# Softmax attention on TensorE: full 128-row products against two 64-row halves in two PSUM banks, with transposes moved between them

## The chip, the cores and the metric

One core of a Trainium2 chip runs the whole kernel, which is one launch of a two-layer transformer. The metric is the device time in microseconds (us), lower is better. The kernel before took 1138.88 us as the median of three runs (1138.76 to 1141.35).

## What is computed

The reference is two layers on 1024 tokens of width 256: softmax attention with 16 heads (4 key/value heads), a squared-relu mixture of experts, linear attention, and a silu mixture of experts, each with a layer norm ahead and a residual sum behind. The change is in the first of the four:

```
xq = (x @ wq + bq).reshape(B, S, 16, 128)
xk = (x @ wk + bk).reshape(B, S, 4, 128);  xv = (x @ wv + bv).reshape(B, S, 4, 128)
attn = softmax(einsum('bqhgd,bkhd->bhgqk', (xq / sqrt(128)).reshape(B, S, 4, 4, 128), xk))
out = einsum('bhgqk,bkhd->bqhgd', attn, xv).reshape(B, S, 2048)
return out @ wo + bo
```

## The kernel before

`softmax_attention_phase` (L223) goes through the four key/value heads one after another, a lap each. Every product is made in float32 precision out of three float32r products of high and low parts: `product` (L37) issues high x high (L39), high x low (L40) and low x high (L41).

Inside a lap the work is written as a list of events, which every engine walks in the same order and takes its own part of:

- `("q", h)` is the projection of one query head, `("k",)` and `("v",)` those of keys and values, `("y", b)` the output projection of half of the tokens.
- `("s", n)` is half of a tile of scores: 128 queries by 512 keys (L521). Two of them fill a slot of two PSUM banks. VectorE then takes the maximum (L686), ScalarE the exponential into `prob` (L579), VectorE the reciprocal of the sum (L647), and GpSimd multiplies by it (L422).
- `("t", n)` is one step of transposing the probabilities: four transposes of 128x128 from four tiles into one PSUM bank (L531 to L539). ScalarE copies the bank to `pt_h` (L612), VectorE subtracts that from the bank and gets the low part `pt_l` (L697).
- `("p", n)` adds one block of 128 keys to the outputs of 512 queries (L540): three products with `v` as weights and `pt` streaming. After eight of them the output unit is copied to `o_h` (L622) and `o_l` (L703).

A lap has 64 steps of each of s, t and p. The scores run 12 steps ahead of the rest (`LEAD`). The steady part of the list (L252 to L259) is a period of s, s, p, p, t, t, repeated, with a `q` ahead of every eighth pair; in it t is 4 steps ahead of p. Behind it follows `change` (L261), the passage to the next head with its k, v and y, or `closing` (L266) in the last lap.

What holds the engines together are semaphores. `turned(j)` (L325) gives the transposes two banks, one for a step, so a step waits until the one before the last is split (L535). `pt_h` and `pt_l` are rings of four steps (`PT`), so ScalarE's copy of step n waits until `("p", n - 4)` is done (L611). The slots of scores are two in the laps; a slot is free for the next scores when its exponential is done. The wait counts on `pt_split` and `pv_done` have `LIFT` added, which is given to the semaphore at the start.

## Time and profile before

| | |
|---|---|
| median of three runs | 1138.88 us |
| the profiled execution, its own time | 1144.78 us |
| its span (first to last instruction) | 1142.9 us |
| mean granted TensorE clock | 0.973 |
| TensorE products busy (6276 instructions) | 1059.6 us, 93% |
| weight loads busy | 893.9 us, 78% |
| VectorE, ScalarE, GpSimd busy | 751.3, 599.2, 564.3 us |
| the attention's transposes, first and last start | 40.8 and 602.4 us |

The span is some 2 us shorter than the execution's own time, and that is 5.9 us above the median. The attention takes roughly the first 610 us of the span. Start times in the rows are us from the start of the span. A product's record is longer than the distance to the next one, since products are pipelined: what a product costs in a dense row of them is read from start to start.

### The profile page before, as it was taken

What the parts mean: (1) busy time and instruction counts of PE and PEld (TensorE: products, weight loads), DVE (VectorE), ACT (ScalarE), POOL (GpSimd) and SP (SyncE); (2) the same over time, 40 slices, a digit from 0 to 9 for tenths busy, and PEclk for the clock granted to TensorE, in tenths of its full rate; (3) what the DMA queues carried; (4) which work ended last, traced back from release to release, by engine and by line L of the source; (5) the groups of instructions that cost most, each with busy time, mean ns of one, the idle gap of its engine ahead of it and who ended that gap; (6) DMA issues with size and microseconds to landing.
All of it is one profiled execution on the core that took longest, in us unless ns stands there. A gap on an engine that the chain in (4) does not pass through costs nothing. (4 is left out here: it accounts for less than half of the span.)

```text
span 1142.9 us, 16866 instructions
## 1 busy us (share of the span) xinstructions
PE 1059.6 (93%) x6276; PEld 893.9 (78%) x6276; DVE 751.3 (66%) x1312; ACT 599.2 (52%) x1027; POOL 564.3 (49%) x408
## 2 busy tenths in 40 slices
PE   5899999999999999999998899997977978999992
PEld 4788888888888888888886776654755778999992
DVE  4877665777457775667775644446778765777777
ACT  3566654666446665456662424333422255777772
POOL 1664623756136563355540347772314776644453
PEclk9999999999999999999999899999988998999997
DMA  8400210002501672000001146631200457666665
GB/s 198 49 29 1 54 40 1 19 10 46 48 1 40 209 216 52 1 1 1 1 1 39 43 146 217 212 125 55 106 2 5 157 190 239 205 226 222 224 208 203
DMA packets 45634, 109.84 MB, mean 96 GB/s; under 512 B 8519, under 2 KB 26069, under 8 KB 43504
## 3 DMA queue, kind: packets, MB, share of 16 engines
q1 hardware_dynamic: 38640, 95.46, 29.1%
q0 software_dynamic: 6912, 13.30, 3.1%
q8 instruction: 50, 0.82, 0.3%
q14 instruction: 32, 0.26, 0.1%
HBM read 94.27 MB, written 41.29 MB: 119 GB/s over the span
## 5 line engine op out<-in xcount | busy, mean ns | idle before, releaser
L422 POOL TENSOR_TENSOR at_prob<-at_prob,at_inv_sum 128x1024 f32<-128x1024 f32 x128 | 243.6, 1905 | 286.4 <-DVE at_inv_sum L647 286.4
L612 ACT ACTIVATE at_pt_h<-ps 128x512 fp32r<-128x512 f32 x256 | 139.1, 596 | 152.4 <-PE ps L537 152.3
L697 DVE TENSOR_TENSOR at_pt_l<-ps,at_pt_h 128x512 fp32r<-128x512 f32 x256 | 164.6, 685 | 64.5 <-ACT at_pt_h L612 64.5
L686 DVE TENSOR_REDUCE at_neg_max<-ps 128x1 f32<-128x1024 f32 x128 | 154.7, 1209 | 36.3 <-PE ps L41 35.9
L579 ACT ACTIVATE at_prob<-ps,at_neg_max 128x1024 f32<-128x1024 f32 x128 | 143.6, 1122 | 17.9 <-DVE at_neg_max L686 17.9
L537 PE MATMUL ps<-ident,at_prob 128*128 128x128 f32 x1024 | 133.8, 274 | 3.8 <-POOL at_prob L422 3.8
L2072 POOL DMA_INDIRECT lines<-f_y,f_x_raw x96 | 97.1, 1011 | 81.0 <-ACT f_y L1990 51.9
L537 PEld LDWEIGHTS ps<-ident,at_prob 128*128 128x128 f32 x1024 | 120.1, 141 | 21.1 <-POOL at_prob L422 4.7
L39 PE MATMUL ps<-at_k_h,at_q_h 128*128 128x512 f32 x256 | 109.0, 426 | 0.0
L39 PE MATMUL ps<-at_pt_h,at_v_h 128*128 128x512 f32 x256 | 101.1, 395 | 0.0
L41 PE MATMUL ps<-at_pt_h,at_v_l 128*128 128x512 f32 x256 | 100.8, 394 | 0.0
L41 PE MATMUL ps<-at_k_h,at_q_l 128*128 128x512 f32 x256 | 100.8, 394 | 0.0
L40 PE MATMUL ps<-at_k_l,at_q_h 128*128 128x512 f32 x256 | 100.6, 393 | 0.0
L40 PE MATMUL ps<-at_pt_l,at_v_h 128*128 128x512 f32 x256 | 100.2, 392 | 0.0
L1023 POOL TENSOR_TENSOR f_act<-f_act,f_cw_row 128x1024 f32<-128x1024 f32 x32 | 77.5, 2424 | 35.8 <-DVE f_act L1058 29.2
L1058 DVE SCALAR_TENSOR_TENSOR f_act<-ps,f_relu 128x1024 f32<-128x1024 f32 x34 | 41.6, 1223 | 57.2 <-ACT f_relu L964 57.2
L964 ACT ACTIVATE f_relu<-ps 128x1024 f32<-128x1024 f32 x36 | 36.8, 1022 | 72.4 <-PE ps L41 72.4
L39 PE MATMUL ps<-f_x_h,f_e_h 128*128 128x384 f32 (+1 forms) x192 | 67.1, 349 | 3.9 <-DVE f_x_l L2188 2.0
L41 PE MATMUL ps<-f_x_h,f_e_l 128*128 128x384 f32 (+1 forms) x192 | 64.8, 338 | 0.0
L40 PE MATMUL ps<-f_x_l,f_e_h 128*128 128x384 f32 (+1 forms) x192 | 64.8, 337 | 0.0
L2059 POOL DMA_INDIRECT slots<-f_row,f_slot_of x48 | 51.1, 1065 | 20.1 <-issue 13.1
L926 PE MATMUL ps<-f_act,f_e_raw 128*128 128x512 f32 x128 | 59.7, 593 | 0.0
(308 smaller groups left out, 2546.7 us busy)
## 6 DMA issues: line engine op xcount, KB each, us to landing
e_raw<-in_we SPq DMA_DIRECT2D x32, 624.0 KB, 4.2
f_cw_row<-cw SPq DMA_DIRECT2D x32, 512.0 KB, 3.9
slots<-in_empty SPq DMA_DIRECT2D x4, 3456.0 KB, 43.9
f_x_raw<-slots SPq DMA_DIRECT2D x32, 432.0 KB, 4.8
lines<-in_empty SPq DMA_DIRECT2D x3, 2048.0 KB, 32.8
f_e_raw<-in_we SPq DMA_DIRECT2D x32, 128.0 KB, 2.2
at_wq_raw<-in_wq SPq DMA_DIRECT2D x4, 512.0 KB, 3.7
at_wo_raw<-in_wo SPq DMA_DIRECT2D x4, 512.0 KB, 3.5
```

Source lines behind the costliest of these rows:

```text
L39: nc.tensor.matmul(out, lhs_h, rhs_h, start=start, stop=False)
L40: nc.tensor.matmul(out, lhs_h, rhs_l, start=False, stop=False)
L41: return nc.tensor.matmul(out, lhs_l, rhs_h, start=False, stop=stop)
L422: nc.gpsimd.tensor_tensor(prob[:, t % RING, :], prob[:, t % RING, :], inv_sum[:, t:t + 1].broadcast_to([P, T]), ALU.mult).then_inc(normed, 1)
L537: last = nc.tensor.transpose(turned(e[1])[:, i * P:(i + 1) * P], prob[:, (4 * u + i) % RING, kt * P:(kt + 1) * P], net.ident[:, :])
L579: nc.scalar.activation(halves(prob[:, t % RING, :]), slot(k, start), ACT.Exp, bias=neg_max[:, t:t + 1], accum_out=row_sum[:, t:t + 1]).the ...
L612: nc.scalar.activation(pt_h[:, e[1] % PT, :], turned(e[1]), ACT.Copy).then_inc(pt_high, 1)
L686: nc.vector.tensor_reduce(neg_max[:, t:t + 1], slot(n, start), AX.XY, ALU.max, negate=True).then_inc(maxed, 1)
L697: nc.vector.tensor_tensor(pt_l[:, e[1] % PT, :], turned(e[1]), pt_h[:, e[1] % PT, :].bitcast(F32), ALU.subtract).then_inc(pt_split, 1)
L926: last = nc.tensor.matmul(ps[:, 4 + b, :], e_raw[:, m, 1, :], act_of(m)[:, cols], start=first, stop=final)
L1023: nc.gpsimd.tensor_tensor(act_of(r), act_of(r), cw_row[:, r % ROWS, :], ALU.mult).then_inc(weighed, 1)
L2072: nc.gpsimd.indirect_dma_start(out=net.lines, out_offset=bass.IndirectOffsetOnAxis(ap=line_of, axis=0), in_=y[:, n % YRING, b, :], in_offs ...
```

## The change

Every attention product in the laps is taken apart into two halves of its contraction: rows 0 to 63 and rows 64 to 127 of weights and of what streams. `half_products` issues the halves in pairs, one on each half of the rows, into two different PSUM banks; in the first turn half 0 goes to bank 0 and half 1 to bank 1, in the second turn crosswise. The second turn waits until the first one is done (`halved`). One `s` event is now one turn over a whole tile of 1024 keys, one `p` event one turn over two steps, each with 256 of the queries in a bank; q, k, v and y in the laps are split into a first turn and a rest `("r", ...)`. The transposes read 64 rows each: eight to a step, each with 64 columns of the identity streaming, and bank `h` gets the queries of half `h` for both steps of a pair. So a bank is whole only after the second step of a pair, and the first step waits until both banks of the pair before are split. The ring `pt` is still four steps, now as two pairs. The steady period becomes s, t, s, p, t, p. The finished outputs go through `o_full` in SBUF.

The core of the diff (bare ... lines mark what is left out):

```diff
+HROWS = P // 2
+def upper(r):
+    return slice(r * HROWS, (r + 1) * HROWS)
+def half_products(nc, turn, outs, lhs_h, lhs_l, rhs_h, rhs_l, start, stop):
+    passes = [(lhs_h, rhs_h), (lhs_h, rhs_l), (lhs_l, rhs_h)]
+    for n, (lhs, rhs) in enumerate(passes):
+        for r in range(2):
+            j = r ^ turn
+            last = nc.tensor.matmul(outs[j], lhs[j][upper(r)], rhs[j][upper(r)], start=start and turn == 0 and n == 0,
+                                    stop=stop and turn == 1 and n == len(passes) - 1)
+    return last
...
+    def woven(a, b):
+        return [a[0], b[0], a[1], b[1]]
+    def query(s):
+        return ("q", (s // 2 + 2) // TT) if (s // 2 + 2) % TT == 0 and s < STEPS else None
+    opening = [("k",), ("q", 0), ("v",), ("s", 0)]
+    for s in range(2, LEAD, 2):
+        opening += [("s", s), ("s", s - 1)]
+    opening += [("s", LEAD - 1), ("vs",)] + pair("t", 0)
+    steady = woven([query(LEAD), rest(*query(LEAD))], pair("s", LEAD))
     for s in range(LEAD, STEPS, 2):
-        if (s // 2 + 2) % TT == 0:
-            steady.append(("q", (s // 2 + 2) // TT))
-        steady += pair("s", s)
+        ahead = query(s + 2)
+        begun, ended = ([ahead], [rest(*ahead)]) if ahead else ([], [])
+        turn = pair("t", s - LEAD + 2)
         if s > LEAD:
-            steady += pair("p", s - LEAD - 2)
-        steady += pair("t", s - LEAD + 2)
+            (s0, s1), (p0, p1) = pair("s", s), pair("p", s - LEAD - 2)
+            steady += [s0, turn[0], s1, p0] + begun + [turn[1], p1] + ended
+        else:
+            steady += begun + turn + ended
...
-    change = [("k",)] + pair("p", at) + pair("t", at + 4) + [("v",)] + pair("p", at + 2) + pair("t", at + 6)
+    change = woven([("k",), rest("k")], pair("p", at)) + pair("t", at + 4)
+    change += woven([("v",), rest("v")], pair("p", at + 2)) + pair("t", at + 6)
     for n in range(3):
-        change += pair("s", 2 * n) + pair("p", at + 4 + 2 * n) + pair("t", at + 8 + 2 * n)
-    change += pair("s", 6) + pair("p", at + 10) + pair("s", 8) + pair("p", at + 12)
-    change += [("vs",)] + pair("s", 10) + [("y", 0)] + pair("t", 0) + [("y", 1)]
+        change += woven(pair("s", 2 * n), pair("p", at + 4 + 2 * n)) + pair("t", at + 8 + 2 * n)
+    change += woven(pair("s", 6), pair("p", at + 10)) + woven(pair("s", 8), pair("p", at + 12))
+    change += [("vs",)] + pair("s", 10) + [("y", 0)] + pair("t", 0) + [rest("y", 0), ("y", 1), rest("y", 1)]
     closing = []
     for n in range(at, STEPS, 2):
-        closing += pair("p", n) + (pair("t", n + 4) if n + 4 < STEPS else [])
+        closing += woven(pair("p", n), pair("t", n + 4)) if n + 4 < STEPS else pair("p", n)
...
-        pt_h, pt_l = sb("pt_h", [P, PT, BANK], F32R), sb("pt_l", [P, PT, BANK], F32R)
+        pt_h, pt_l = sb("pt_h", [P, PT // 2, 2, BANK], F32R), sb("pt_l", [P, PT // 2, 2, BANK], F32R)
         o_h, o_l = sb("o_h", [P, PER, T], F32R), sb("o_l", [P, PER, T], F32R)
+        o_full = sb("o_full", [P, BANK])
...
-        def turned(j):
-            return ps[:, 4 + j % 2, :]
-        def o_bank(u):
-            return ps[:, 6 + u % 2, :]
+        def turned(h):
+            return ps[:, 4 + h, :]
+        def stored(pt, step):
+            return pt[:, step // 2 % (PT // 2), step % 2, :]
+        def moving(pt, step):
+            return [pt[:, step // 2 % (PT // 2), h, step % 2 * D:(step % 2 + 1) * D] for h in range(2)]
+        def queries(ap):
+            return ap.rearrange("p (i h q) -> p h i q", i=4, h=2)
+        def outputs(h):
+            return ps[:, 6 + h, 0:D]
+        def all_outputs():
+            return ps[:, 6:8, 0:D].rearrange("p h (i q) -> p h i q", i=4)
...
+                        if turn:
+                            pe.wait_ge(halved, halves_of[g, job])
+                            place_ = slot(slot_of[job], start)
...
-                            keys = slice(b * BANK, (b + 1) * BANK)
-                            last = product(nc, slot(n, start)[:, b, :], q_h[:, hh % 2, i * P:(i + 1) * P],
-                                           q_l[:, hh % 2, i * P:(i + 1) * P], k_h[:, keys], k_l[:, keys], True, True)
-                            if b == 1:
+                            keys = [slice(j * BANK, (j + 1) * BANK) for j in range(NB)]
+                            if b:
+                                pe.wait_ge(halved, halves_of[g, ("s", 2 * t)])
+                            at_ = slot(slot_of["s", 2 * t], start)
+                            last = half_products(nc, b, [at_[:, j, :] for j in range(NB)],
+                                                 [q_h[:, hh % 2, i * P:(i + 1) * P]] * NB, [q_l[:, hh % 2, i * P:(i + 1) * P]] * NB,
+                                                 [k_h[:, j] for j in keys], [k_l[:, j] for j in keys], True, True)
+                            if b:
                                 last.then_inc(s_full, 1)
+                            else:
+                                half_done(last, g, e)
...
-                            pe.wait_ge(pt_split, LIFT + own * STEPS + e[1] - 1)
+                            if kt % 2 == 0:
+                                pe.wait_ge(pt_split, LIFT + own * STEPS + e[1])
                             for i in range(4):
-                                last = nc.tensor.transpose(turned(e[1])[:, i * P:(i + 1) * P],
-                                                           prob[:, (4 * u + i) % RING, kt * P:(kt + 1) * P], net.ident[:, :])
-                            last.then_inc(pt_full, 1)
+                                at = kt % 2 * D + i * HROWS
+                                for h in range(2):
+                                    last = nc.tensor.transpose(turned(h)[:, at:at + HROWS],
+                                                               prob[upper(h), (4 * u + i) % RING, kt * P:(kt + 1) * P],
+                                                               net.ident[upper(h), upper(h)])
+                            if kt % 2:
+                                last.then_inc(pt_full, 2)
...
+                            turn = e[1] % 2
                             if e[1] == 0:
                                 pe.wait_ge(v_split, g + 1)
-                            if kt == 0:
-                                pe.wait_ge(o_split, LIFT + g * UNITS + u - 1)
-                            pe.wait_ge(pt_split, LIFT + g * STEPS + e[1] + 1)
-                            keys = slice(kt * P, (kt + 1) * P)
-                            product(nc, o_bank(u), v_h[:, keys], v_l[:, keys], pt_h[:, e[1] % PT, :], pt_l[:, e[1] % PT, :],
-                                    kt == 0, kt == KT - 1).then_inc(pv_done, 1)
-                        if e[0] == "y":
-                            if e[1] == 0:
+                            if turn:
+                                pe.wait_ge(halved, halves_of[g, ("p", e[1] - 1)])
+                            elif kt:
+                                pe.wait_ge(pv_done, LIFT + g * STEPS + e[1])
+                            elif g * UNITS + u:
+                                pe.wait_ge(o_moved, 2 * (g * UNITS + u) - 1)
+                            if not turn:
+                                pe.wait_ge(pt_split, LIFT + g * STEPS + e[1] + 2)
+                            for step in (e[1] - turn, e[1] - turn + 1):
+                                kt = step % KT
+                                keys = slice(kt * P, (kt + 1) * P)
+                                last = half_products(nc, turn, [outputs(0), outputs(1)], [v_h[:, keys]] * 2, [v_l[:, keys]] * 2,
+                                                     moving(pt_h, step), moving(pt_l, step), kt == 0, kt == KT - 1)
+                            if turn:
+                                last.then_inc(pv_done, 2)
+                            else:
+                                half_done(last, g, e)
...
+                        if e[0] == "t" and e[1] % 2:
                             if start == 0:
                                 exps()
...
+                        if e[0] == "p" and e[1] % 2 and events[place - 1][0] == "t":
+                            exps()
...
+                        if e[0] == "t" and e[1] % 2:
+                            for h in range(2):
+                                for w in waiting:
+                                    w[2] += 1
+                                inverts(3)
+                                lows()
+                                dve.wait_ge(pt_high, own * STEPS + e[1] + h)
+                                nc.vector.tensor_tensor(stored(pt_l, e[1] - 1 + h), turned(h), stored(pt_h, e[1] - 1 + h).bitcast(F32),
+                                                        ALU.subtract).then_inc(pt_split, 1)
+                            output_low()
```

The halves of q, k, v and y are issued in the same way as those of s. In the opening the events of each tile of scores are set one behind those of the next, and GpSimd waits for its weights' split with one wait in place of another.

## Rows read from the trace of the kernel before

**Rows 1.** The page, busy time, share of the span, instructions, by engine
```profile
PE 1059.6 (93%) x6276; PEld 893.9 (78%) x6276; DVE 751.3 (66%) x1312; ACT 599.2 (52%) x1027; POOL 564.3 (49%) x408
```

**Rows 2.** Busy time by stretch; columns: stretch, length, busy per engine, TensorE clock, DMA
```profile
51.00:72.00 21.00, 21.00 (x118) 17.94 (x117) 16.04 (x28) 13.56 (x25) 16.61 (x14) 1.00 0.09 26
```

**Rows 3.** Timeline of TensorE, one steady period; columns: start us, length us, instruction
```profile
65.44 1.03 PE L537 MATMUL ps<-ident,at_prob 128*128 128x128 f32 x8
66.23 0.48 PE L39 MATMUL ps<-at_k_h,at_q_h 128*128 128x512 f32 x1
...
67.70 0.39 PE L39 MATMUL ps<-at_pt_h,at_v_h 128*128 128x512 f32 x1
...
69.06 1.04 PE L537 MATMUL ps<-ident,at_prob 128*128 128x128 f32 x8
```

**Rows 4.** Timeline of ScalarE in the same period
```profile
66.07 1.09 ACT L612 ACTIVATE at_pt_h<-ps 128x512 fp32r<-128x512 f32 x2 [1.32 <-PE ps L537]
67.04 1.12 ACT L579 ACTIVATE at_prob<-ps,at_neg_max 128x1024 f32<-128x1024 f32 x1
```

**Rows 5.** Timeline of VectorE in the same period
```profile
66.70 1.29 DVE L697 TENSOR_TENSOR at_pt_l<-ps,at_pt_h 128x512 fp32r<-128x512 f32 x2 [0.64 <-ACT at_pt_h L612]
...
68.36 1.20 DVE L686 TENSOR_REDUCE at_neg_max<-ps 128x1 f32<-128x1024 f32 x1
```

**Rows 6.** Groups of TensorE by line and shape, the attention's transposes and their weight loads
```profile
L537 PE MATMUL ps<-ident,at_prob 128*128 128x128 f32 x1024 | 133.8, 274 | 3.8 <-POOL at_prob L422 3.8
L537 PEld LDWEIGHTS ps<-ident,at_prob 128*128 128x128 f32 x1024 | 120.1, 141 | 21.1 <-POOL at_prob L422 4.7 <-issue 0.2 <-DVE at_pt_l L697 0.2
```

**Rows 7.** Timeline, start of transposes after a wait for GpSimd, window 594.6:594.8
```profile
592.68 1.89 POOL L422 TENSOR_TENSOR at_prob<-at_prob,at_inv_sum 128x1024 f32<-128x1024 f32 x1 [1.69 <-DVE at_inv_sum L647]
...
594.63 0.20 PEld L537 LDWEIGHTS ps<-ident,at_prob 128*128 128x128 f32 x2 [0.78 <-POOL at_prob L422]
```

**Rows 8.** Line L1336 of linear attention: products over 32 rows, four banks
```profile
L1336 PE MATMUL ps<-la_q_p,la_k_t x128: 372/375/792, 798.7 to 849.8; 32*128 32x256 f32 x128
```

**Rows 9.** Timeline, one burst of L1336: its first 0.2 us, and the whole
```profile
814.77 0.31 PEld L1336 LDWEIGHTS ps<-la_q_p,la_k_t 32*128 32x128 f32 x8 [0.20 <-issue]
814.77 0.50 PE L1336 MATMUL ps<-la_q_p,la_k_t 32*128 32x256 f32 x4
...
814.77 1.15 PE L1336 MATMUL ps<-la_q_p,la_k_t 32*128 32x256 f32 x16
```

**Rows 10.** Timeline of TensorE, full products of 256 columns in a dense row
```profile
817.36 0.28 PE L39 MATMUL ps<-shared_h,xn_h 128*128 128x256 f32 x1
817.48 0.28 PE L40 MATMUL ps<-shared_l,xn_h 128*128 128x256 f32 x1
```

**Rows 11.** Timeline, the last product of an output unit and the copy that waits for it
```profile
585.73 0.39 PE L41 MATMUL ps<-at_pt_h,at_v_l 128*128 128x512 f32 x1
...
586.16 0.60 ACT L622 ACTIVATE at_o_h<-ps 128x512 fp32r<-128x512 f32 x1 [1.00 <-PE ps L41]
```

**Rows 12.** Timeline of TensorE, a projection of queries (12 products) and the scores behind it
```profile
73.49 0.48 PE L39 MATMUL ps<-xn_h,at_wq_h 128*128 128x512 f32 x1
...
76.38 0.39 PE L39 MATMUL ps<-at_k_h,at_q_h 128*128 128x512 f32 x1
```

**Rows 13.** Timeline of TensorE, first product of `change` and first of the next lap
```profile
147.24 0.48 PE L39 MATMUL ps<-xn_h,at_wkv_h 128*128 128x512 f32 x1
...
190.66 0.40 PE L39 MATMUL ps<-xn_h,at_wq_h 128*128 128x512 f32 x1
```

**Rows 14.** Timeline of TensorE in `closing`, one period
```profile
590.39 0.48 PE L39 MATMUL ps<-at_pt_h,at_v_h 128*128 128x512 f32 x1
...
592.65 0.47 PE L39 MATMUL ps<-at_pt_h,at_v_h 128*128 128x512 f32 x1
```

**Rows 15.** Busy time by stretch, two stretches in which TensorE stood for part of the time
```profile
37.00:47.00 10.00, 6.52 (x27) 5.36 (x26) 7.07 (x9) 4.62 (x9) 8.92 (x5) 0.83 0.49 67
780.00:797.00 17.00, 10.87 (x51) 6.67 (x50) 11.40 (x32) 8.93 (x17) 5.92 (x7) 1.00 0.21 73
```

More of the change, by code:

```diff
@@ L249, in pair, with rest @@
         return [(kind, s), (kind, s + 1)]
-    opening = [("k",), ("q", 0), ("v",)] + [("s", s) for s in range(LEAD)] + [("vs",)] + pair("t", 0)
-    steady = []
+    def rest(*e):
+        return ("r", e)
+    def woven(a, b):
[5 more added lines that the diff above has]
+        opening += [("s", s), ("s", s - 1)]
@@ L356, in laps @@
                 run(g, steady + change, first)
-            run(KV - 1, [e for e in steady if e != ("q", PER)] + closing, first)
+            run(KV - 1, [e for e in steady if e not in (("q", PER), rest("q", PER))] + closing, first)
         def belongs_next(events, n):
@@ L465, in _, with half_done @@
             def _(pe):
+                first_halves = count()
+                halves_of = {}
+                def half_done(last, g, e):
+                    halves_of[g, e] = next(first_halves) + 1
+                    last.then_inc(halved, 1)
                 def run(g, events, start):
+                    slot_of = {}
                     jobs = jobs_of(events)
@@ L499, in run @@
                             n += 1
-                        if e[0] in "kq":
+                            slot_of[e] = n
+                        job = e[1] if e[0] == "r" else e
+                        turn = int(e[0] == "r")
+                        done = whole(events, e)
+                        if turn:
+                            pe.wait_ge(halved, halves_of[g, job])
+                            place_ = slot(slot_of[job], start)
+                        elif e in jobs:
+                            place_ = slot(n, start)
@@ L513, in run @@
[L513 to L520 removed]
+                            cols = [slice(b * BANK, (b + 1) * BANK) for b in range(NB)]
@@ new lines, in run @@
+                            for c in range(DC):
+                                hh = slice(job[1] % PER * DH, (job[1] % PER + 1) * DH) if job[0] == "q" else None
+                                wt = (wkv_h[:, 0, c, :], wkv_l[:, 0, c, :]) if job[0] == "k" else (wq_h[:, c, hh], wq_l[:, c, hh])
+                                if done == e:
+                                    for b in range(NB):
+                                        last = product(nc, place_[:, b, :], *wt, xn_h[:, c, cols[b]], xn_l[:, c, cols[b]],
+                                                       c == 0, c == DC - 1)
+                                else:
+                                    last = half_products(nc, turn, [place_[:, b, :] for b in range(NB)], [wt[0]] * NB, [wt[1]] * NB,
+                                                         [xn_h[:, c, b] for b in cols], [xn_l[:, c, b] for b in cols],
+                                                         c == 0, c == DC - 1)
@@ L556, in run @@
                                 for hh in range(PER):
-                                    last = product(nc, tokens_of(slot(n, start), i), o_h[:, hh, toks], o_l[:, hh, toks],
-                                                   wo_h[:, hh, :], wo_l[:, hh, :], hh == 0, hh == PER - 1)
-                            last.then_inc(y_full, 1)
+                                    if done == e:
+                                        for b in range(NB):
+                                            last = product(nc, tokens_of(place_, spot[b]), o_h[:, hh, toks[b]], o_l[:, hh, toks[b]],
+                                                           wo_h[:, hh, :], wo_l[:, hh, :], hh == 0, hh == PER - 1)
+                                    else:
+                                        last = half_products(nc, turn, [tokens_of(place_, k) for k in spot],
+                                                             [o_h[:, hh, k] for k in toks], [o_l[:, hh, k] for k in toks],
+                                                             [wo_h[:, hh, :]] * NB, [wo_l[:, hh, :]] * NB,
+                                                             i == hh == 0, (i, hh) == (TT // 4 - 1, PER - 1))
@@ L561, in _ @@
+                            if done:
+                                last.then_inc(y_full, 1)
+                            else:
+                                half_done(last, g, e)
                 for s in lifted["pe"]:
@@ L570, in run @@
                 def run(g, events, start):
+                    slot_of = {}
                     waiting = []
```

137 lines of the change are left out of this document (80 added, 57 removed).

## Prediction

> **What bounds the kernel now.** The page first: TensorE is busy 93% of the span, no other engine over 66% [rows 1]. The busy time by stretch then says whether that holds where the change is made: from 51 to 72 us TensorE is busy in all of the 21.00 us, at full clock, VectorE 16.04, ScalarE 13.56, GpSimd 16.61 [rows 2]. So a steady period is as long as TensorE's work in it, 69.06 - 65.44 = 3.62 us, and in it 8 transposes take 0.79, the 6 products of scores 1.47, the 6 of outputs 1.36 [rows 3]. The timelines of the other engines show what must fit behind it: from the moment the transposes are there, ScalarE copies two banks in 1.09 us, then takes the exponential, 1.12 [rows 4], and VectorE's second subtraction ends at 66.70 + 1.29 = 67.99, 1.92 after ScalarE's start at 66.07 [rows 4, 5]. The next transposes start at 69.06, so this evacuation has 1.07 us to spare. It is this slack that the new order must be held against.
>
> **TensorE's own work after the change.** The number of products doubles and each has half of the rows, so all hangs on two halves running at once. The trace has such products, over 32 rows and four banks: eight weight loads start within 0.31 us and four products run side by side from 814.77 [rows 9]. The burst of 16 has its last start 1.15 - 0.375 = 0.775 behind the first [rows 8, 9]; less one load of 0.11 (eight loads of 0.185 each in 0.31, two sets of four: the second set starts about 0.11 late) that is three rounds of 0.216 each. I take these rounds for halves too, as the nearest rows.
> - Scores: a row of full products costs 1.36 / 6 = 0.227 each [rows 3], a pair of halves 0.216. Six pairs a period: 1.30.
> - Outputs: twelve pairs of 256 columns. Full products of 256 columns are 0.12 apart [rows 10], half a round is 0.108; I take 0.112: 1.34.
> - Transposes: 0.79 + 0.08 of exposed load behind them, 8 to a period [rows 3]. After a wait the second load starts 0.20 - 0.14 = 0.06 behind the first [rows 6, 7], so loads are not what spaces them at 0.109; it is the 128 columns, and the new ones stream 64. I take 0.06 a pair, 8 pairs: 0.48, and keep 0.109 as the upper bound, since no row shows a 64-column one. The first product behind a group waits for its weights, 0.11 less the transpose beside it.
>
> Left alone TensorE would need about 3.2 us for 3.62. A page of the Trainium skill speaks against even this: "TensorE: Matmul & The Clock Gate", Part 3, has a weight load overlap a running product only where the row groups differ. The rows of before disagree for full products: 0.227 apart with a load for each leaves no room for a load of 0.11 on top of 512 columns. By the page's rule each pair of halves would pay its load; that is a rival below.
>
> **The loop that the new order closes.** The period is s0, t0, s1, p0, t1, p1. Three waits in the diff make a ring. (1) t0 of a period waits until both banks of the pair before are split. (2) Both copies to `pt_h` come only behind t1, as each bank holds both steps. (3) The copies also wait for `pv_done` of the pair four steps back, as `PT` is still 4; that pair is p0, p1 of the same period, and p1 now stands behind t1 on TensorE. Before, p stood ahead of t, so that (3) was fulfilled on arrival, and each step had its own bank. Behind t0, everything of TensorE is queued: it takes instructions in order, and only s0 lies between p1 and that wait.
>
> From the end of the last subtraction to the same point one period on:
> - signal to first load 0.05 (592.68 + 1.89 to 594.63 [rows 7]); t0: first load 0.06, three more pairs 0.18, weights for s1 0.11: together 0.40;
> - s1, three pairs of 0.216: 0.65; p0, six of 0.112: 0.67;
> - t1: 0.24, and 0.06 until p1 has its weights or sees p0 done: 0.30;
> - p1 to the start of its last pair 0.56, its end 0.28 [rows 10], ScalarE's start 0.04 (585.73 + 0.39 to 586.16 [rows 11]): 0.88;
> - copies and subtractions, unchanged in shape: 1.92.
>
> Sum 4.82 us against 3.62. The other queues fit: VectorE's maximum (1.20 [rows 5]) starts some 1.3 into the loop, the subtractions at 3.5; ScalarE's exponential lies behind its copies, from -0.83 to 0.5; s0, 0.65, fits into the 2.2 in which TensorE would wait, of which about 1.4 stay idle. GpSimd's multiplication, 1.9, is used two periods later. At the end of an output unit the extra copy through `o_full` delays the exponential by 0.6 and the maximum still finds it; its subtraction stands behind those of the pair. These cost nothing under cover of the idle TensorE; without it they would be ScalarE's 0.6 every fourth period.
>
> **The sum.** A lap has 25 such periods (s from 14 to 62), four laps 100: 100 x 1.20 = +120 us.
> - Queries: 2.89 before [rows 12]. After, the first turn (1.30) is on the loop, the second in the idle part; the next s0 waits for the exponential at about 6.7, so t0 comes about 1.2 late, and VectorE's low part of q may push the subtractions by 0.5. About +0.2 each, 12: +3.
> - Start of a lap: 18 pairs of halves and 8 transposes in place of full ones, about -0.6, four times: -2.
> - `change`, 43.42 before [rows 13], has s, p, s, p, t, t, where 2.6 lies between t1 and the next t0 and 2.2 is needed, so no ring: transposes 6 x 0.3, scores, outputs, k, v and y together about 1.8, less 0.4 for the rest of y, which waits for its own first turn. About -3.2, three times: -10.
> - `closing`, 2.26 a period before [rows 14], is p, t, p, t: 0.40 + 0.67 + 0.18 + 0.29 + 1.92 = 3.46, five times +1.2: +6.
> - Opening: the first maximum comes one turn later, +0.6; smaller edits 0.
>
> Sum +117: the profiled execution's 1144.78 would become 1262, and from the median, 5.9 lower, 1138.9 + 117 = **1256 us**.
>
> **Bounds.** With transposes at 0.109 (+0.25 a loop), outputs at 0.12 (+0.1), scores at 0.227 (+0.03) and ScalarE 0.1 after a product's end (+0.06), the loop is 5.26: +44, and `change` gains some 8 less: 1308. Transposes hidden wholly, outputs at 0.108 and the weights behind them for nothing: 4.6, so -22: 1234.
>
> **Rivals.**
> - *Faster: the ring does not bind*, as the order on TensorE would leave the copies and subtractions enough time. It is decided at 3.62: beside TensorE's 2.53 of the ring all the rest would have to fit in 1.09, where it is 0.05 + 0.04 + 0.28 + 1.92 = 2.29. Then 100 x (3.2 - 3.62) - 12 = 1085 us. The lighter TensorE work speaks for it, rows 4 and 5 against it: 4%.
> - *A shorter ring*: copies start behind t1, not p1. Loop 0.40 + 0.65 + 0.67 + 0.18 + 0.29 + 1.92 = 4.11: +46, so 1185. Against it speaks L611 with `PT` unchanged: 5%.
> - *Dearer halves*: loads exposed, as the page has it, or halves one after another. With a load of 0.11 for each of the ring's 15 pairs of products +1.65: 1420. Halves in turn add 0.65 + 0.67 + 0.67 + 0.48 = 2.5 to the ring: about 1500. The four side by side in rows 9 speak against both: 4%.
> - *The clock falls*, from 2.4 to 1.2 GHz. From 37 to 47 us, with TensorE busy 6.52 of 10, it has 0.83 granted; from 780 to 797, with 10.87 of 17, it has 1.00 [rows 15]; the new period would be busy about 70% of the time. All of it slow would add 2.5 a loop: up to 1500. 7%, mostly in part.
> - *Nothing to measure*: gain and ring cancel; the ring would have to be 3.7 long. 1%.
>
> **The numbers.** Forecast 79%, its own range 1232 to 1308. The range takes in most of that and the nearer part of the clock case: 1215 to 1320; the shorter ring at 1185, the dear and the fast cases are left out. A change of this kernel can be told from none at about 0.3%, 3.4 us. Slower 0.94, same 0.01, faster 0.05.
>
> **What would show it.** The period from t0 to t0 near 4.8 and constant; TensorE or its loads idle some 1.4 us ahead of t0, released by VectorE's `pt_l`; ScalarE's `pt_h` released by the product of outputs, no longer by the transposes; starts of scores in pairs 0.216 apart; a group of 8 half transposes in about 0.24; `change` about 40 us long. TensorE's share falls to about 80%. The forecast is wrong if the period is 3.2 (no ring), 4.1 (the wait on p1 does not bind), or if pairs of halves are over 0.25 apart.

## The result, and the profile after

The changed kernel took **1320.16 us** as the median of four runs (1315.98 to 1323.90), beside 1140.12 for the kernel before on the same chip: a ratio of 1.158, 95% interval 1.1535 to 1.1617. So it is slower by 180 us. The forecast was 1256, the range 1215 to 1320: the sign and the place of the loss are as predicted, its size is half as large again as the sum of 117, and the median lies on the upper edge of the range.

The page of the kernel after, busy time and instructions by engine, and its queue of instructions (packets, MB, share of the DMA engines):

```profile
PE 1075.3 (82%) x11020; PEld 910.5 (69%) x11020; DVE 759.3 (58%) x1312; ACT 614.9 (47%) x1059; POOL 566.9 (43%) x408
...
q8 instruction: 87, 1.43, 0.4%
```

TensorE's busy time is nearly that of [rows 1], its share is down from 93% to 82%: the time that was added is time in which it stands. One steady period in the timeline, the answer to [rows 3 to 5] (start us, length us, instruction, idle before and what ended it):

```profile
64.78 0.47 PE L647 MATMUL ps<-ident,at_prob 64*128 64x64 f32 x8 [1.47 <-DVE at_pt_l L855]
...
65.03 0.51 PE L61 MATMUL ps<-at_k_h,at_q_h 64*128 64x512 f32 x2
65.34 0.43 PE L61 MATMUL ps<-at_k_l,at_q_h 64*128 64x512 f32 x2
65.56 0.44 PE L61 MATMUL ps<-at_k_h,at_q_l 64*128 64x512 f32 x2
65.79 0.33 PE L61 MATMUL ps<-at_pt_h,at_v_h 64*128 64x256 f32 x2
...
66.51 0.44 PE L647 MATMUL ps<-ident,at_prob 64*128 64x64 f32 x8
66.77 0.39 PE L61 MATMUL ps<-at_pt_h,at_v_h 64*128 64x256 f32 x2
...
67.46 0.28 PE L61 MATMUL ps<-at_pt_h,at_v_l 64*128 64x256 f32 x2
67.58 0.40 PE L61 MATMUL ps<-at_k_h,at_q_h 64*128 64x512 f32 x2
67.82 0.40 PE L61 MATMUL ps<-at_k_l,at_q_h 64*128 64x512 f32 x2
67.85 1.09 ACT L751 ACTIVATE at_pt_h<-ps 128x512 fp32r<-128x512 f32 x2 [2.96 <-PE ps L61]
68.05 0.39 PE L61 MATMUL ps<-at_k_h,at_q_l 64*128 64x512 f32 x2
68.48 1.29 DVE L855 TENSOR_TENSOR at_pt_l<-ps,at_pt_h 128x512 fp32r<-128x512 f32 x2 [1.22 <-ACT at_pt_h L751]
...
69.83 0.46 PE L647 MATMUL ps<-ident,at_prob 64*128 64x64 f32 x8 [1.38 <-DVE at_pt_l L855]
```

The ring can be read off it: t0 at 64.78, s1 at 65.03, p0 at 65.79, t1 at 66.51, p1 at 66.77 to 67.46, ScalarE's copies at 67.85, released by the product of outputs (L61), VectorE's second subtraction to 68.48 + 1.29 = 69.77, t0 again at 69.83. That is 5.05 us from t0 to t0, where the kernel before took 3.62; the 83 periods of the laps that hold no query are 5.07 on average (5.01 to 5.15). The next scores have been issued from 67.58, and then TensorE stands for 1.38 us. The groups by line and shape say that this holds for all the laps (busy us, mean ns | idle us before, by releaser):

```profile
L751 ACT ACTIVATE at_pt_h<-ps 128x512 fp32r<-128x512 f32 x256 | 138.8, 594 | 331.8 <-PE ps L61 281.5
L647 PE MATMUL ps<-ident,at_prob 64*128 64x64 f32 x2048 | 109.2, 229 | 142.6 <-DVE at_pt_l L855 138.1
```

Before, the transposes waited 3.8 us in all [rows 6]; now 142.6, of which 138.1 for `pt_l`.

A second, smaller loss was in no step of the prediction. The timeline of SyncE's queue in the kernel after, ahead of the end of lap 1:

```profile
155.72 0.52 SPq L455 DMA_DIRECT2D lines<-in_empty  x1
```

The timeline of TensorE at the end of that lap:

```profile
182.33 0.80 PE L61 MATMUL ps<-xn_h,at_wq_h 64*128 64x512 f32 x2 [7.02 <-issue]
```

Busy time by stretch there (stretch, length, busy of PE, PEld, DVE, ACT, POOL, granted clock, DMA share, GB/s):

```profile
174.00:182.00 8.00, 1.31 (x24) 1.03 (x20) 1.45 (x3) 2.18 (x4) 1.89 (x1) 0.82 0.81 70
182.40:187.00 4.60, 4.60 (x32) 3.67 (x34) 0.00 (x0) 1.67 (x2) 0.00 (x0) 0.61 0.68 68
182.40:185.00 2.60, 2.60 (x12) 2.10 (x14) 0.00 (x0) 0.00 (x0) 0.00 (x0) 0.50 0.77 68
```

TensorE stands for 7.02 us and the profile shows nothing that it waits for. In this stretch the DMA engines are 0.81 busy with a fill of 2 MB that was issued at 155.72 (L455, a part of the expert layer's preparation that the change does not touch). TensorE was busy 1.31 us of the 8.00 from 174 to 182. Behind the stall the granted clock is 0.50, the level of 1.2 GHz, until 185.0; from 187.0 to 200 it is 1.00 again, the level of 2.4 GHz. The 0.61 of the longer stretch is a mean of the two.

Where the profiled execution's +175.3 went (1320.05 against 1144.78): the four steady laps +163.9 (45.5, 43.3, 37.3, 37.8; 25 periods at 5.07 for 3.63 on average make 36 of each), the three changes of head +1.7, the closing with its output projection +9.9, the opening +1.2, all behind the attention -1.5.

### The profile page after: what moved, and what is told of

The parts are those of the page before. It is cut to its first block and busy times, and to the rows that moved or that the text cites. A ratio compares the mean times of both kernels' runs of the same rounds, so it can differ in the third digit from the quotient of the medians.

```text
span 1318.2 us, 26383 instructions
## 1 busy us (share of the span) xinstructions
PE 1075.3 (82%) x11020; PEld 910.5 (69%) x11020; DVE 759.3 (58%) x1312; ACT 614.9 (47%) x1059; POOL 566.9 (43%) x408
## 5 line engine op out<-in xcount | busy, mean ns | idle before, releaser
L647 PE MATMUL ps<-ident,at_prob 64*128 64x64 f32 x2048 | 109.2, 229 | 142.6 <-DVE at_pt_l L855 138.1
L647 PEld LDWEIGHTS ps<-ident,at_prob 64*128 64x128 f32 x2048 | 92.8, 140 | 185.0 <-DVE at_pt_l L855 130.8
L61 PE MATMUL ps<-at_pt_h,at_v_h 64*128 64x256 f32 x1024 | 161.4, 305 | 0.9 <-ACT at_o_full L762 0.4
L61 PE MATMUL ps<-at_pt_h,at_v_l 64*128 64x256 f32 x1024 | 149.3, 281 | 0.0
L61 PE MATMUL ps<-at_pt_l,at_v_h 64*128 64x256 f32 x1024 | 148.9, 281 | 0.0
L61 PE MATMUL ps<-at_k_h,at_q_h 64*128 64x512 f32 x512 | 115.0, 442 | 9.5 <-ACT at_prob L715 9.3
L61 PEld LDWEIGHTS ps<-at_pt_h,at_v_h 64*128 64x128 f32 x1024 | 102.1, 189 | 6.9 <-PE ps L61 1.2
L61 PEld LDWEIGHTS ps<-at_pt_l,at_v_h 64*128 64x128 f32 x1024 | 102.1, 189 | 5.4
L61 PE MATMUL ps<-at_k_l,at_q_h 64*128 64x512 f32 x512 | 103.4, 395 | 2.5 <-issue 2.5
L61 PE MATMUL ps<-at_k_h,at_q_l 64*128 64x512 f32 x512 | 103.3, 394 | 0.0
L61 PEld LDWEIGHTS ps<-at_pt_h,at_v_l 64*128 64x128 f32 x1024 | 101.9, 189 | 0.0
## 6 DMA issues: line engine op xcount, KB each, us to landing
slots<-in_empty SPq DMA_DIRECT2D x4, 3456.0 KB, 43.4
```

Source lines behind the costliest of these rows:

```text
L61: last = nc.tensor.matmul(outs[j], lhs[j][upper(r)], rhs[j][upper(r)], start=start and turn == 0 and n == 0, stop=stop and turn == 1 and n ...
L647: last = nc.tensor.transpose(turned(h)[:, at:at + HROWS], prob[upper(h), (4 * u + i) % RING, kt * P:(kt + 1) * P], net.ident[upper(h), upp ...
```

## The experiments

### The ring: take the wait on p1 away

`e1_ring8` is the changed kernel with a ring of eight steps in place of four; room for it comes from laying two buffers over one that is dead by then.

```diff
-    PT = 4
+    PT = 8
```

> The kernel after with the ring of probabilities twice as long (8 steps), so that the copies of a pair of transposes no longer wait for p1 of the same period; the room for it comes from laying the buffers of the projection and of the values over the centred input. Ring of waits (my theory): the loop loses p1 but keeps the copies behind t1 and t0 behind the split: 0.06 + 0.27 + 0.77 + 0.72 + 0.18 + 0.27 + 1.92 = 4.19 us a period where the kernel after has 5.04, 100 periods, so some 84 us less, about 1236. Rival, that halves of a product or the issue of so many instructions set the period: no change, 1320.

Measured: 1253.15 us (1252.57 to 1253.74, 2 runs), ratio 1.094 (1.0899 to 1.0984). Its timeline of TensorE has t0 of three periods at

```profile
62.81 0.46 PE L647 MATMUL ps<-ident,at_prob 64*128 64x64 f32 x8 [0.62 <-DVE at_pt_l L855]
...
67.00 0.47 PE L647 MATMUL ps<-ident,at_prob 64*128 64x64 f32 x8 [0.52 <-DVE at_pt_l L855]
...
71.20 0.47 PE L647 MATMUL ps<-ident,at_prob 64*128 64x64 f32 x8 [0.53 <-DVE at_pt_l L855]
```

that is 4.19 and 4.20 apart, to the hundredth what the ring without p1 was to give. So the wait on `pv_done` was worth 0.85 us a period, and t0, s1, p0, t1 and the evacuation still make a ring of their own. The time is 17 above the 1236 that was expected. Two stalls without a releaser, 9.5 and 11.6 us, stand where the fills run: 21 us, where the changed kernel has 9.5, so they account for some 12 of the 17.

### The order: put both turns of the transposes together

`e2_together` keeps `PT` at 4 and all the halves, and changes the steady list alone, so that both t come behind all of p, as in the kernel before.

```diff
-            steady += [s0, turn[0], s1, p0] + begun + [turn[1], p1] + ended
+            steady += [s0, p0, s1] + begun + [p1] + ended + turn
```

> The kernel after with the steady period in the order s0, p0, s1, p1, t0, t1, halves of products and banks as they are. Ring theory: 2.8 us of products lie between t1 and the next t0, where 2.2 are needed, so the period is TensorE's own 1.40 + 1.43 + 0.46 + 0.08 = 3.4 us, 166 us less than after; with what the changes of head and the closing cost more, about 1130 to 1150. Rival, halves or instruction issue set the period: it stays above 4.5, over 1260.

Measured: 1211.58 us (1203.75 to 1214.21), ratio 1.056 (1.0507 to 1.0605). The undisturbed period is 3.35, as expected, and shorter than the 3.62 of the kernel before: the order, not the halves, makes the ring. But the time is 62 us above the range that was expected. Every fourth period, at the end of an output unit, is 4.5:

```profile
61.37 0.65 PE L647 MATMUL ps<-ident,at_prob 64*128 64x64 f32 x15
...
64.72 0.66 PE L647 MATMUL ps<-ident,at_prob 64*128 64x64 f32 x15
...
66.73 0.62 ACT L765 ACTIVATE at_o_h<-at_o_full 128x512 fp32r<-128x512 f32 x1
67.25 1.07 ACT L751 ACTIVATE at_pt_h<-ps 128x512 fp32r<-128x512 f32 x2
67.87 1.29 DVE L855 TENSOR_TENSOR at_pt_l<-ps,at_pt_h 128x512 fp32r<-128x512 f32 x2 [2.28 <-ACT at_pt_h L751]
...
69.22 0.71 PE L647 MATMUL ps<-ident,at_prob 64*128 64x64 f32 x16 [0.92 <-DVE at_pt_l L855]
```

ScalarE copies the outputs out, takes an exponential, copies the outputs' high part (66.73), and only then the transposes (67.25), though these started on TensorE at 64.72 and took 0.65. The copies through `o_full` cost nothing while TensorE stood 1.4 us a period; without that cover they cost over 1 us each. Queries do the same, and the fills' stalls are 9.5 and 12.0 us here.

### The order alone, without halves

`e3_order_full` is the kernel before (full products, one bank to a step) with only the events of the steady list in the changed kernel's order. `e5_order_full_ring8` is the same with `PT` 8.

```diff
-        steady += pair("s", s)
+        turn = pair("t", s - LEAD + 2)
...
-            steady += pair("p", s - LEAD - 2)
-        steady += pair("t", s - LEAD + 2)
+            (s0, s1), (p0, p1) = pair("s", s), pair("p", s - LEAD - 2)
+            steady += [s0, turn[0], s1, p0, turn[1], p1]
```

> The kernel before (full products, a bank for each step of transposes) with the new order s0, t0, s1, p0, t1, p1 in the steady part. Ring theory: the order does harm only with a pair in two banks; here t0 waits for the split of t0 of the last period, which is copied behind p0, so the period stays 3.62 to 3.75: 1138 to 1152. Rival, the order alone costs the time (the copies wait for the outputs): 4.5 or more, over 1220.

Measured: 1215.78 us (1214.36 to 1217.19, 2 runs), ratio 1.062 (1.0572 to 1.0658). My theory, that the order costs only together with banks filled over two steps, fell.

> The kernel before with the new steady order (as e3) and, this time, a ring of 8 steps in place of 4. e3 cost 72 us where I had expected none. Theory now: with a ring of four the copies wait for p0 and p1, which stand behind their transposes in this order, and the exponential, the reciprocal and the multiplication of the tile queue up behind the late copies, so that t0 of the next unit waits for GpSimd. Then the longer ring gives most of it back: 1140 to 1165. Rival: the order itself costs the time, since t0 stands one score and two outputs earlier than before and needs its four tiles multiplied by then; then it stays near 1215.

Measured: 1189.67 us (1189.57 to 1189.77, 2 runs), ratio 1.042 (1.0373 to 1.0460), between the two theories. The group of the transposes by line and shape in e3:

```profile
L539 PE MATMUL ps<-ident,at_prob 128*128 128x128 f32 x1024 | 152.6, 276 | 61.6 <-POOL at_prob L424 50.0 <-DVE at_pt_l L699 11.7
```

The same group in e5:

```profile
L539 PE MATMUL ps<-ident,at_prob 128*128 128x128 f32 x1024 | 152.7, 276 | 40.8 <-POOL at_prob L424 32.0 <-DVE at_pt_l L699 8.8
```

e3 loses 70 us against the kernel before that ran beside it (1145.88), e5 48 (against 1142.14). So the ring of four is worth some 22 us of the loss, and 48 stay with eight steps. The largest wait of both is one that I had left out: in the kernel before t closes the period, in the new order t0 comes right behind s0, so the first transposes of an output unit want GpSimd's product (1.9 us, behind ScalarE's exponential and VectorE's reciprocal) most of a period earlier. In e3 t0 waits 1.82 us for it at 77.53. In the changed kernel this wait does not show in the laps: there t0 waits longer for `pt_l`.

### Halves in the transposes alone

`e4_turns_only` takes e2's order with all products full (rows 0 to 127); only the transposes read 64 rows.

```diff
-                            last = half_products(nc, b, [at_[:, j, :] for j in range(NB)],
...
+                            last = product(nc, at_[:, b, :], q_h[:, hh % 2, i * P:(i + 1) * P], q_l[:, hh % 2, i * P:(i + 1) * P],
+                                           k_h[:, keys], k_l[:, keys], True, True)
```

> The kernel after with only the transposes in halves of 64 rows: scores, outputs and projections are full products, no first turn and rest, order s, s, p, p, t, t. If what the change gains lies in the transposes alone: 1.36 + 1.41 + 0.46 + 0.1 = 3.33 a period where before has 3.62, 29 us less over 100 periods, so 1108 to 1120. Rival, going from products over 128 rows to products over 64 and back costs TensorE time (0.1 to 0.2 each way, twice a period): 1130 to 1150. Second rival, halves of the products gain beside full ones: then this one is slower than the run with all in halves and the transposes together.

Measured: 1204.92 us (1196.20 to 1208.67), ratio 1.053 (1.0494 to 1.0568), far above what was expected. It too waits for `pt_l` behind the copies at the end of an output unit, 33.7 us in all, and it stalls for 3.74 and 1.60 us beside fills. And its undisturbed period is 3.65 against 3.35 in e2, though a full product costs no more than two halves. The timeline of TensorE, the 16 transposes of a period and the scores behind them, in e4:

```profile
62.65 0.71 PE L643 MATMUL ps<-ident,at_prob 64*128 64x64 f32 x16
63.29 0.50 PE L39 MATMUL ps<-at_k_h,at_q_h 128*128 128x512 f32 x1
```

The same in e2:

```profile
72.64 0.66 PE L647 MATMUL ps<-ident,at_prob 64*128 64x64 f32 x16
73.10 0.48 PE L61 MATMUL ps<-at_k_h,at_q_h 64*128 64x512 f32 x2
```

From 64-row transposes to 128-row products 0.64 us pass, to 64-row ones 0.46; about 0.1 more stands ahead of the transposes in e4. Passing from full to half products and back so costs some 0.3 us a period, about what the half transposes save (0.79 before, 0.47 for 16 of them now). A page of the Trainium skill, "TensorEngine Tiling (Array Packing)", Key Properties, says that changing the tiling mode drains TensorE; e4's 0.64 against 0.46 agrees. So the halved products gain nothing themselves, but are what lets the halved transposes keep their gain.

### The stalls without a releaser: move the fills

`e6_fills_late` is the changed kernel with all three fills of `lines` behind the load of the last head's `wo`.

```diff
+                sp.wait_ge(wo_split, 1 + 4 * (KV - 1))
+                sp.dma_start(wo_raw[:, :, :], net.dram["wo"][KV - 1]).then_inc(wo_loaded, 16)
+                for g in range(KV - 1):
                     sp.dma_start(net.lines.rearrange("(g r) d -> g r d", g=KV - 1)[g],
...
-                sp.wait_ge(wo_split, 1 + 4 * (KV - 1))
-                sp.dma_start(wo_raw[:, :, :], net.dram["wo"][KV - 1]).then_inc(wo_loaded, 16)
```

> The kernel after, with the three fills of the lines table moved from the laps to the start of the last lap. In the profile of after TensorE stands for 7.0 us at 175 and 1.8 us at 366 with nothing to wait for, each time while such a fill holds the DMA engines. Theory: TensorE waits for its instructions, whose loading shares the DMA engines with the fill; then the stalls at 175 and 366 are gone and one of the kind shows in the last lap or none; time equal to after or up to 15 us less. Rival, the stalls are TensorE's own (a longer program, whatever the DMA does): they stay where they were.

Measured: 1341.81 us (1339.26 to 1344.37, 2 runs), ratio 1.175 (1.1697 to 1.1801). The edit did not put the fills where the expectation had them: SyncE reaches this place in the third lap, and the change to the last head starts only at 593.53. The timeline of SyncE's queue:

```profile
449.37 37.14 SPq L458 DMA_DIRECT2D lines<-in_empty  x3
```

The stalls at 175 and 366 us are gone; in the timeline of TensorE the waits longer than 2 us between 470 and 560 us are

```profile
485.88 0.37 PE L648 MATMUL ps<-ident,at_prob 64*128 64x64 f32 x2 [11.35 <-issue]
...
512.26 0.48 PE L648 MATMUL ps<-ident,at_prob 64*128 64x64 f32 x4 [10.03 <-issue]
...
535.24 0.58 PE L61 MATMUL ps<-at_pt_h,at_v_l 64*128 64x256 f32 x1 [8.84 <-issue]
```

The stalls follow the fills, which refutes the rival that they are TensorE's own and stay where they were. That it would be no dearer was wrong: 30 us of stalls in one lap in place of the 9.5 beside the fills of the changed kernel, and the difference is about the 22 us by which it is slower.

What TensorE waits for can be read from the DMA queues by window. Queue 8 holds 87, 64 and 50 packets of 16 KB in the kernels with 11020, 8068 (e4) and 6276 products; worked out from their MB, that is an estimated 65 bytes for each product and each weight load in all three, so it is taken here for the queue of TensorE's instructions. In the changed kernel it has a packet about every 11 us. Here are the queues (packets, MB, share of the DMA engines) in the windows 153.3:180.1, in which it has none, and 180.1:181.3; TensorE goes on at 182.33:

```profile
q1 hardware_dynamic: 1720, 2.14, 65.1%
...
q8 instruction: 1, 0.02, 5.0%
```

It is so everywhere: in all the runs, each stall of over 1.4 us without a releaser in the attention ends 0.9 to 1.6 us after the end of a packet of this queue, and ahead of each one of 7 us and more the queue had started no packet for 23 to 30 us. So the instructions come late. It is not the busy DMA engines alone that delay them. In the window 468:532 of the changed kernel another fill (`slots`, 3.4 MB a piece) holds the engines at 0.95; the queue gets its packets, and TensorE has no such stall:

```profile
q1 hardware_dynamic: 1694, 14.44, 94.5%
q8 instruction: 5, 0.08, 0.6%
```

And e6's stall that ends at 512.26 has a DMA share of 0.21 beside it (busy time by stretch):

```profile
502.00:512.00 10.00, 0.23 (x3) 0.09 (x3) 0.16 (x1) 1.10 (x3) 1.89 (x1) 0.63 0.21 76
```

What the long stalls have in common is a fill of `lines`, in packets of 1 KB. Why it holds up the packets of instructions, no run shows.

### Mending the version with the turns together

`e7_together_late_high` is e2 with ScalarE's copies of the transposes ahead of the outputs' high part, VectorE's `o_l` a period later and its low parts behind its subtractions, the query's first turn behind t and its rest behind the next s0, and `closing` as p, p, t, t.

```diff
-            steady += [s0, p0, s1] + begun + [p1] + ended + turn
+            steady += [s0] + ended + [p0, s1, p1] + turn + begun
...
+                            exps()
+                            while late:
+                                o_high(late.pop())
```

> e2 with three orders changed: ScalarE copies the transposes ahead of o_h at the end of an output unit, the first turn of q stands behind the transposes and its rest behind the next s0, closing is p, p, t, t. In e2 TensorE waited some 50 us for the split behind those copies. Theory: these waits go, and the period is 3.4 throughout: about 45 us less than e2 and 8 from the closing and the changes, 1150 to 1165. Rival: the waits come back elsewhere (the low part of q, GpSimd's multiplication): less than 20 us gained.

Measured: 1163.27 us (1160.65 to 1165.20), ratio 1.018 (1.0147 to 1.0219), 48 below e2, as expected. Two stalls remain beside fills, 9.94 and 9.92 us. `e8_fills_paced` adds one thing, each fill in eight pieces of 256 KB spread over the lap:

```diff
-                    sp.dma_start(net.lines.rearrange("(g r) d -> g r d", g=KV - 1)[g],
...
+                    for n in range(8):
+                        sp.wait_ge(exped, g * TILES + 3 * n + 6)
+                        sp.dma_start(net.lines.rearrange("(g n r) d -> g n r d", g=KV - 1, n=8)[g, n],
```

> e7 with each fill of the lines table cut into eight pieces, each behind three more exponentials. In e2 TensorE stood 9.5 and 12.0 us without a releaser during the fills, and the clock was at 1.2 GHz for 10 and 14 us behind them. Theory (instructions come late while a fill holds the DMA engines): each stall shrinks to the length of a piece, so 20 to 35 us less than e7, 1120 to 1140, which would be at or below the kernel before. Rival (TensorE's own): no change against e7.

Measured: 1141.72 us (1137.78 to 1146.52, 12 runs), ratio 0.9995 (0.9977 to 1.0014): 21.5 less than e7. The two stalls, 19.9 us, are gone, and one of 2.81 remains at 457 us, beside the fill of `slots`. Queue 8 now has a packet at least every 12.5 us from 60 to 620 us, where e7 has gaps of 25.6 and 25.9 ahead of its two stalls. At par with the kernel before.

`e9_query_first` takes one more wait from it. In e8 the scores behind a query wait for the exponential that holds their slot, so the period behind a query puts p0 and the query's rest ahead of s0:

```diff
-            steady += [s0] + ended + [p0, s1, p1] + turn + begun
+            steady += ([p0] + ended + [s0, p1, s1] if ended else [s0, p0, s1, p1]) + turn + begun
```

> This is e8_fills_paced with one more edit: in the period behind the query's first turn the order is p0, the rest of the query, s0, p1, s1, t0, t1, so that s0 starts at least 2.5 us after the transposes before it, when the exponentials that hold its slot are done. In e8 s0 waits about 1.07 us there and the query costs 2.46 + 1.40 us. Theory (what the query costs beyond its own products is the wait for ScalarE's exponentials): about 0.5 us less in each of some 25 periods, so -12 us against e8's 1141.72: 1125 to 1135, faster than both kernels by 0.5 to 1.3%. Rival (the wait only moves: p1 and s1 then stand later, the copies of t0 come late in the next period): 1138 to 1150, no gain.

Measured: **1133.56 us** (1131.40 to 1141.19, 8 runs), ratio 0.992 (0.9893 to 0.9946), the one version that beats both kernels. The timeline of TensorE in e8, the scores behind a query:

```profile
75.21 0.50 PE L61 MATMUL ps<-at_k_h,at_q_h 64*128 64x512 f32 x2 [0.82 <-ACT at_prob L723]
```

What is left of it in the timeline of e9:

```profile
84.65 0.49 PE L61 MATMUL ps<-at_k_h,at_q_h 64*128 64x512 f32 x2 [0.52 <-DVE at_q_l L818]
```

The gain is 8 us, and not 12 as expected. The 12 were 25 periods at 0.5, and the periods had been miscounted: there are 11. Each becomes 1.14 shorter (6.16 for 7.30), 12.5 in all. Behind eight of them the head's first scores give part of it back as a new wait of 0.52 for `q_l`, and the period they stand in becomes 4.11 for 3.43. That leaves 7. The page of e9 shows TensorE at 92% again, with its busy time 20 us below [rows 1]:

```profile
PE 1039.5 (92%) x11020; PEld 924.4 (82%) x11020; DVE 750.9 (66%) x1312; ACT 618.1 (55%) x1059; POOL 564.1 (50%) x408
```

### Paced fills in the two original kernels

The same edit of the fills, alone, in the kernel before and in the changed one.

> The kernel before with one edit: each fill of lines is cut into eight pieces that are spread over the lap, as in e8. The kernel before shows only one stall of 1.53 us at 306.47 beside a fill. Theory (the stalls come from instruction loading beside a full DMA, and before has few of them): 0 to 5 us less, 1137 to 1142. Rival (spreading the fills gives any version of this kernel the 21 us that it gave e7): about 1120.

Measured: 1140.87 us (1137.96 to 1143.90), ratio 0.998 (0.9965 to 0.9999), 2 us less.

> The changed kernel with the same one edit: each fill of lines cut into eight pieces spread over the lap. After's profile shows stalls without a releaser of 7.02, 1.83 and 0.66 us beside fills and a low clock behind them. Theory (part of the loss is instruction loading beside a full DMA, the rest is the ring of copies): 10 to 20 us less, 1300 to 1310. Rival (the ring has slack enough to take the stalls up, or the pieces bring stalls of their own): 1316 to 1325, as after.

Measured: 1308.38 us (1303.54 to 1313.36), ratio 1.142 (1.1388 to 1.1450): 12 less than the changed kernel by the medians, and 18 by the ratios, since the kernel before took 1143.06 beside this run and 1140.12 beside the changed kernel. So the fills account for 12 to 18 of its 180 us, with the low clock behind the stalls; in the kernel before they cost 2. And e9's gain over the kernel before is not its fills: against `e10_before_paced` it still is 7 us faster.

## Why the prediction was right, and where it was off

- **The ring.** Right in all its three waits: t0 released by `pt_l`, the copies released by the outputs, TensorE idle 1.38 to 1.47 ahead of t0 (forecast 1.4). e1 shows the third wait by itself, 5.05 to 4.19 (4.82 to 4.11 by the prediction's terms).
- **The size of the loop**, 5.05 for 4.82. The subtraction ahead of t0 ended at 64.64, so this turn of the ring, to 69.77, is 5.13. From 64.64, t0 and s1 take 1.15 to 65.79, for 0.40 + 0.65 = 1.05: t0 starts 0.14 behind the subtraction, where it is 0.06 behind it at 69.83. p0 takes 66.51 - 65.79 = 0.72 for 0.67, t1 66.77 - 66.51 = 0.26 for 0.30. The term that was mis-sized is the last one, "p1 to the start of its last pair 0.56, its end 0.28, ScalarE's start 0.04: 0.88", which measures 67.85 - 66.77 = 1.08: the last pair starts 0.69 behind the first, and ScalarE 0.11 behind the modelled end of 67.46 + 0.28. The evacuation is the 1.92 that was taken. At 5.07 on average the difference is some +24 us over 100 periods more than the +120 of the forecast. It lies inside the bound of 5.26 that the prediction gave.
- **Halves of products.** The step that failed is the price of a pair: I took 0.216 from rounds of products over 32 rows [rows 9], and the halves cost what full products cost, 0.23 for 512 columns and 0.12 for 256. That it came so near is luck. Those rows stream 256 columns, not 512, and plain float32, not float32r. And the terms as written, 0.775 less 0.11 over three, give 0.222. So q, k, v and y gain nothing either. The rival of exposed loads is refuted: the rule in the Trainium skill, "TensorE: Matmul & The Clock Gate", Part 3, held neither for full products nor for halves, both 0.23 apart. TensorE's natural period is e2's 3.35, not 3.2.
- **Transposes.** Right: eight half transposes and the load behind them in 0.25 (forecast 0.24).
- **`change`.** Forecast -10 in all, measured +1.7: 46.10, 44.6 and 44.6 us where the kernel before has 43.4, 46.8 and 43.4. The transposes' gain there is real, but the halves' gain of 1.8 was not, and the output projection waits for the chain through `o_full`, `o_h` and `o_l`:

```profile
226.24 0.39 PE L61 MATMUL ps<-at_wo_h,at_o_h 64*128 64x256 f32 x2 [1.46 <-DVE at_o_l L795]
```

- **`closing`.** The periods are as forecast (3.48 from 763.13 to 766.61, for 3.46). The rest of its +9.9 for +6 is the projection behind it: it starts after a wait of 2.17, and from 783.3 to 786.5, in which TensorE is busy throughout, the granted clock is 0.51.

```profile
763.13 0.46 PE L647 MATMUL ps<-ident,at_prob 64*128 64x64 f32 x8 [1.31 <-DVE at_pt_l L855]
...
766.61 0.46 PE L647 MATMUL ps<-ident,at_prob 64*128 64x64 f32 x8 [1.23 <-DVE at_pt_l L855]
```

- **The missing term.** I counted the added instructions (16866 to 26383) as starts on TensorE and not as code to be loaded. e11 puts this term at 12 us by the medians.
- **The clock.** The rival "all of it slow" did not come. From 60 to 81 us TensorE was busy 15.38 of 21.00 at a granted clock of 1.00; where it fell in the attention, as from 182.4 to 185.0 and from 783.3 to 786.5, it was for a short stretch behind a stall or a wait.
- **What no rival named.** That p1 must stay ahead of the copies was read rightly, but e3 and e5 show that the order costs 48 us even with a ring of eight steps and full products; 32.0 us of it stand as waits for GpSimd's product. Had the ring been shorter, this would have been the next wait, and no rival named it.
- **What was luck.** The range went up to 1320 for the case of a low clock. That case did not come; the time got to its edge by the fills' stalls, by `change` and by a longer loop, and the first had no term. The mechanism held, but the width of the range did the rest.

Together: loop +24, `change` +12, closing +4 and the fills +12 make 52 of the 58 us that the forecast of +117 lacked in the profiled execution (+175.3). The rest, about 6, was not told apart; it is no more than the two readings of the fills' term, 12 and 18, differ by.

## What to carry to other kernels

When a change moves work between two steps of an in-order queue, list for each buffer who must free it and who must fill it, and sum the way round: here 4.82 by paper and 5.05 on the chip, while TensorE's own work fell. Halving a contraction over two banks makes a product no cheaper; it paid here only for the transposes, whose halves also stream 64 columns in place of 128, and only where the neighbours on the engine had the same tile shape. For a stall that no instruction releases, look at the packets of the instruction queue and at the big transfer beside them: cut that up, and try it on its own.

## What was not expected of the hardware

- **Full and half products cost the same**: 0.23 us for 512 columns, whether one product over 128 rows or two at once over 64. Half transposes, of 64 columns each, cost 0.06 a pair (four pairs and the load behind them in 0.25) against 0.1 for one full transpose (eight in 0.79).
- **Changing between 64-row and 128-row tiles** costs about 0.3 us a period for the way there and back (e4 against e2).
- **TensorE stalls for 7 to 12 us when its instructions come late**, with nothing in the trace that releases it. Such a stall ends 1.2 to 1.6 us after the end of a packet of 16 KB in queue 8, the first one to start for 23 to 30 us. The stalls move with the fills of `lines` (e6) and go when these are cut up (e8, e11). They are long in the kernels with 11020 products (9.9 us in e7, 87 packets), 3.7 in e4 (64 packets) and 1.53 in the kernel before (50). A high DMA share is neither enough (0.95 beside `slots`, no stall of this size) nor needed (0.21 in e6). What in the fill holds the packets up stays open.
- **The granted clock falls behind such a stall**, to 0.50 from 182.4 to 185.0 in the changed kernel, so each costs more than its length.
